# Attention, then experts, on one core: the values' product, three small transpositions and the output projection moved to other places in TensorE's order

## The reference

```python
def _stablemax3_s(x):
    pos = 1.0 + x * (1.0 + 0.5 * x * (1.0 + x / 3.0))
    neg = 1.0 / (1.0 - x * (1.0 - 0.5 * x * (1.0 - x / 3.0)))
    return jnp.where(x >= 0, pos, neg)
...
x = x + attention(layernorm(x))        # q, k, v, scores, stablemax3, values, output projection
h = silu(xn @ w1[e]) * (xn @ w3[e])    # xn = layernorm(x), four experts e, 512 wide
x = x + sum_e gates[:, e] * (h[e] @ w2[e])   # gates: softmax over the top 2 of 4
```

## Time and profile before

| | |
|---|---|
| time, median of 3 runs | 1129.02 us (1128.45 to 1129.56) |
| the profiled execution | 1130.74 us, of which 1129.0 us from the first instruction to the last |
| granted clock of TensorE, mean | 0.995 of full speed |
| instructions | 29283 |
| busy in the span | PE 98%, DVE 87%, ACT 89%, POOL 66% |
| DMA | 117.49 MB, mean 104 GB/s |

### The profile page before, as it was taken

The page is one execution under the profiler, slowest core; times in us unless marked ns, Lnnn a source line. Parts: engine busy times, 40 slices in busy tenths (PEclk is TensorE's granted clock), DMA queues, the critical chain, the costliest instruction groups (busy, mean ns, idle before and its releaser), DMA issues.

```text
span 1129.0 us, 29283 instructions
## 1 busy us (share of the span) xinstructions
PE 1104.0 (98%) x9968; PEld 936.7 (83%) x9968; DVE 980.8 (87%) x1789; ACT 1004.1 (89%) x1034; POOL 750.7 (66%) x999
## 2 busy tenths in 40 slices
PE   5889999999999999999999999999999999999998
PEld 4768888888888888888888888888888888888888
DVE  4878999999989999999899999999989899998844
ACT  0699999999999999999999999999999999999982
POOL 5346667776766777676687776677767668776530
PEclk8999999999999999999999999999999999999999
DMA  4534333333332233433323343223333322333100
GB/s 119 176 114 151 107 96 94 100 121 122 119 103 91 83 120 119 127 113 97 92 89 121 122 126 107 90 94 101 121 122 117 104 89 84 119 123 124 30 6 11
DMA packets 130127, 117.49 MB, mean 104 GB/s; under 512 B 15492, under 2 KB 124708, under 8 KB 130084
## 3 DMA queue, kind: packets, MB, share of 16 engines
q1 hardware_dynamic: 127876, 113.78, 32.3%
q10 hardware_dynamic: 2208, 3.15, 0.8%
HBM read 94.70 MB, written 21.09 MB: 103 GB/s over the span
## 4 chain that ended last, share of the span: by engine, by line
PE 90%; ACT 4%; DVE 3%; DMA 1%; issue 1%; ACTq 0%; SPq 0%; DVEq 0%
PE banks L1275 33%; PE banks L1548 20%; PE sc L1361 11%; PE banks L1293 10%; PE sc L1531 4%; PE misc L1275 2%; ACT poly L741 2%; PE banks L1582 2%; ACT poly L746 1%; PE misc L1408 1%; PE misc L1426 1%; PE misc L1386 1%; PE banks L1531 1%; PE sc L1275 1%; DVE mx L968 1%
## 5 line engine op out<-in xcount | busy, mean ns | idle before, releaser
L462 POOL TENSOR_TENSOR hid<-hid,gate_all 128x512 f32<-128x512 f32 x240 | 379.2, 1643 | 155.9 <-DMA gate_all<-gate_scratch 139.8
L883 DVE SCALAR_TENSOR_TENSOR poly<-w_sq,sc 128x1024 f32<-128x1024 f32 x252 | 303.7, 1216 | 37.6 <-ACT w_sq L637 37.5
L1275 PE MATMUL banks<-xn_hi,w_hi 128*128 128x256 f32 x976 | 289.3, 296 | 0.2
L1275 PE MATMUL banks<-xn_lo,w_hi 128*128 128x256 f32 x976 | 275.4, 282 | 0.0
L1275 PE MATMUL banks<-xn_hi,w_lo 128*128 128x256 f32 x976 | 274.2, 281 | 0.0
L637 ACT ACTIVATE w_sq<-sc 128x1024 f32<-128x1024 f32 x252 | 255.5, 1029 | 7.3 <-PE sc L1361 3.5
L741 ACT ACTIVATE poly<-poly,two 128x2048 f32<-128x2048 f32 x128 | 252.1, 1991 | 0.4
L1548 PE MATMUL banks<-w_sb,hid 128*128 128x128 f32 x1920 | 246.1, 281 | 0.2 <-POOL hid L462 0.2
L968 DVE TENSOR_REDUCE mx<-sc 128x4 f32<-128x1024 f32 x192 | 229.8, 1213 | 11.5 <-PE sc L1531 10.4
L1548 PEld LDWEIGHTS banks<-w_sb,hid 128*128 128x128 f32 x1920 | 223.3, 191 | 16.4 <-POOL hid L462 0.5
L746 ACT ACTIVATE poly<-poly 128x2048 f32<-128x2048 f32 x128 | 236.8, 1896 | 0.0
(11 more groups left out here) (186 smaller groups left out, 1372.5 us busy)
## 6 DMA issues: line engine op xcount, KB each, us to landing
qk_scratch<-qk_split SPq DMA_DIRECT2D x32, 512.0 KB, 3.1
k_tile<-qk_scratch SPq DMA_DIRECT2D x128, 128.0 KB, 2.5
q_pad<-qk_scratch SPq DMA_DIRECT2D x256, 64.0 KB
q_tile<-qk_scratch SPq DMA_DIRECT2D x124, 128.0 KB, 2.5
k_stack<-qk_scratch SPq DMA_DIRECT2D x124, 128.0 KB
gate_all<-gate_scratch SPq DMA_DIRECT2D x30, 512.0 KB, 4.4
x_in<-in_L_attn_x_dram SPq DMA_DIRECT2D x32, 128.0 KB, 2.1
x_res<-in_L_attn_x_dram SPq DMA_DIRECT2D x32, 128.0 KB, 2.2
```

The lines of the kernel that those rows point to most:

```text
L462: nc.gpsimd.tensor_tensor(h, h, by_token.unsqueeze(1).to_broadcast([128, 2, C, 128]), ALU.mult).then_inc(gated, 1)
L883: nc.vector.scalar_tensor_tensor(poly[:, u, :], w_sq[:, u % 2, :], 3.0, distance_buf(n, u), ALU.add, ALU.mult).then_inc(poly_ok, 1)
L1275: last = nc.tensor.matmul(dst, lhs[a], rhs[b], start=(k == 0), stop=(k == len(terms) - 1))
```

## The change

On TensorE, in the first half: `values` goes behind d0 and d1; `values_T` goes ahead of d4; b3 goes ahead of d5 (it stood behind it); `attention_T` leaves its place between d6 and a6 and goes to the end, ahead of `score(0)`. `output_projection` leaves the end of the first half and goes into the second, between `down(0, 0)` and `down(0, 1)`. On ACT the copy of attn_T leaves its place between square 6 and silu 6 and goes into the second half, behind the table load and ahead of the first logarithm. Instructions, sizes and buffers are the same; DVE's, POOL's and SP's orders are the same. It holds for the steps from 2 to 31.

```diff
@@ block.scalar
+            def attention_T_copied(i, off):
+                m = no(i, off) - 1
+                act.wait_ge(attnT_full, m + 1)
+                after(act, res_full, m)
+                nc.scalar.copy(attn_T[:], misc[:, 0:S]).then_inc(attnT_ok, 1)
...
                     square(6)
-                    attention_T_copied()
                     silu(6)
...
+                if settled(n):
+                    attention_T_copied(i, off)
                 if has(i, off):
                     log_of(0)
@@ block.tensor, first half
                 if settled(n):
-                    values()
                     distance(0)
                     distance(1)
+                    values()
                     weighted_values(i, off - 1, 3)
                     ups(1)
                     distance(2)
@@
                     distance(3)
                     up_b_unit(i, off - 2, 2)
                     up_a_unit(i, off - 2, 3)
+                    values_T()
                     distance(4)
-                    values_T()
                     up_a_unit(i, off - 2, 4)
+                    up_b_unit(i, off - 2, 3)
                     distance(5)
-                    up_b_unit(i, off - 2, 3)
                     up_b_unit(i, off - 2, 4)
                     up_a_unit(i, off - 2, 5)
                     distance(6)
-                    attention_T()
                     up_a_unit(i, off - 2, 6)
                     distance(7)
                     up_b_unit(i, off - 2, 5)
                     up_a_unit(i, off - 2, 7)
                     up_b_unit(i, off - 2, 6)
                     up_b_unit(i, off - 2, 7)
-                    output_projection()
+                    attention_T(i, off)
                     return
@@ block.tensor, second half
                 if settled(n):
                     score(0)
                     down(0, 0)
+                    output_projection(i, off)
                     down(0, 1)
                     score(1)
```

More of the change, by code:

```diff
@@ L669, in values_T_copied @@
                     nc.scalar.copy(o_T[:], pv).then_inc(o_ok, 1)
[L671 to L675, removed]
                 early = isinstance(i, int) and n == 1
@@ L1363, in distances, with attention_T, output_projection @@
                 last.then_inc(w_full, 1)
+            def attention_T(i, off):
+                n = no(i, off)
+                if not has(i, off - 1):
+                    return
+                m = n - 1
+                pe.wait_ge(attn_ok, m + 1)
+                for c in range(C):
+                    last = nc.tensor.transpose(misc[:, c * 128:(c + 1) * 128], attn[:, c, :], ident[:])
+                last.then_inc(attnT_full, 1)
+            def output_projection(i, off):
+                n = no(i, off)
+                if not has(i, off - 1):
+                    return
+                m = n - 1
+                pe.wait_ge(attnT_ok, m + 1)
+                for c in range(C):
+                    last = nc.tensor.matmul(misc[:, c * D:(c + 1) * D], attn_T[:, c * 128:(c + 1) * 128],
+                                            proj_T[:, 3, :], start=True, stop=True)
+                last.then_inc(res_full, 1)
             def first_half(i, off):
```

## The result

The changed kernel takes **1133.28 us** (median of 7 runs, 1132.55 to 1134.25) against 1128.81 us (median of 7 runs, 1128.44 to 1129.56) for the kernel before on the same chip: a ratio of 1.0038, 95% interval 1.0029 to 1.0048. That is 4.5 us slower and above the range given. The profiled execution's span is 1132.5 us (1129.0 before), at a granted clock of 0.997 (0.995 before), so the clock did not make it slower.

A forecast was written before the change was run, and what follows sets the result against it. The prediction took TensorE, 98% busy, to bound the kernel, losing time where loads wait. Its terms, 0.22 − 0.08 − 0.12 = +0.02 us a step, +0.6 us in 30 steps, gave 1129.6 us, range 1125.8 to 1132.8.

The forecast's parts named there:

- They keep step: DVE's adding of the result and later maxima some 0.2 us later, TensorE's later scores 0.22 us later: cost 0.
- the maxima's transfer: At d0, uncovered by moving the values' product: at most 0.03 us in every second step, 0 taken.
- The transpositions leave the gap: Between d6 and a6 their 0.22 us was free; ahead of the scores nothing covers them: +0.22 us a step.
- The projection: Moved between two blocks of D, it takes its 0.45 us there; the 0.09 us change to strips stays: sum 0.
- values_T −0.08 and b3 −0.12: Work ahead of d4 and d5 lets DVE's polynomials finish first: gains of 0.08 and 0.12 us a step.
- d4's sign: Profile sign if right: the next record behind d4 starts 0.46 us behind it.
- ACT's copy: Behind the table load, it lengthens ACT's stretch from silu 7 to square 2 by 0.27 us: cost 0, up to 0.05.
- ACT's stretch as the bound: Rival, chance 0.20: stretch 0.5 us longer, not 0.27, so b2 loses 0.13 us every step: +4.5 us, 1133.5 us.
- the margin that the forecast read for b2: At b2's load, waiting for a hidden: 0.15 us left beyond the semaphore's 0.04.
- The waits for the polynomials at d4 and d5: Rival, chance 0.06: these waits stay, DVE being as late as TensorE: +6.6 us, 1135.6 us.
- The faster rival: Chance 0.16: strip change runs under the transpositions at the end, a4 does not wait for silu 3: −3.6 us, 1125.4 us.
- No load hidden: Rival, chance 0.03: weight loads at d4 and d5 never overlap products, regaining some 0.04 us together: +5.4 us, 1134.4 us.

The follow-up runs named there:

- e5: Kernel before, with the two transpositions of attn done twice in the gap between d6 and a6: 1129.27 us against 1129.39, ratio 0.9999.
- e6: Kernel before, with a second pair of the transpositions at the end of the first half, ahead of the projection: 1135.64 us against 1129.39, ratio 1.0056.
- e7: Kernel before, with only the output projection moved behind the first block of D: 1130.17 us against 1129.39, ratio 1.0008.
- e2: Kernel before, with only values_T ahead of d4 and b3 ahead of d5: 1125.13 us against 1129.29, ratio 0.9966.
- e1: Kernel before, with only the values' product moved behind d0 and d1: 1130.04 us against 1129.29, ratio 1.0006.
- e4: Changed kernel with attention_T alone back between d6 and a6: 1129.83 us against 1129.29 for the kernel before, ratio 1.0006.
- e9: e4 with ACT's copy also back between square 6 and silu 6: 1126.38 us against 1129.06 for the kernel before, ratio 0.9974.

## Why the prediction was wrong

The forecast was +0.02 us a step, the measurement +0.137. The largest term was right. One step of the mechanism failed ("They keep step"), one price that had been seen was set to nothing (the maxima's transfer), and two gains were right in mechanism and too large. By the prediction's own terms:

- **The transpositions leave the gap: +0.22.** Right in mechanism and size: the gap kept its 1.19 us (1.20 in the changed kernel, 1.19 with the work doubled in e5), and the new place costs 0.22 us (P +0.223; e6 +0.216).
- **The projection: 0.** Right for TensorE: P does not change in e7 (5833 to 5834 ns).
- **values_T −0.08 and b3 −0.12: together −0.20.** Right in mechanism, over-sized: −0.152 (e2: −0.151 in the same piece). I had read one step. In the means of 27 steps, from a3's last product to a4's second it is 1.247 us before and 1.194 after, so values_T gave 0.053 and not 0.08; d5 takes 0.565 before and 0.463 after, so b3 gave 0.102 and not 0.12. The work of values_T was also counted as 0.44 us, where the rows have 0.36 (531.88 to 532.24) and 0.35 (532.34 to 532.69). That changed nothing, since the chain through silu 3 is longer than the work either way. The same chain is why d4's sign, 0.46 us to the next record, did not come (0.552 in the mean).
- **DVE's adding: "They keep step: 0."** This step of the argument failed. Its own figures have the projection end at 543.1, 0.1 us behind the 543.00 at which the adding started, and say "some 0.2 us later" without a source for the other 0.1. The adding stood directly behind the first maximum, with no wait, 2.34 us behind b7's last product (540.66 to 543.00). In the changed kernel it is 2.61 (541.51 to 544.12): the projection ends about where the forecast had it (543.38 + 0.61 = 543.99), and DVE, which now waits for it, starts 0.13 us after that. In the means, against b7's last product, the adding is 0.265 us later, the maximum behind it 0.274, and TensorE's second scores 0.227. DVE falls 0.047 us behind TensorE, in e7 0.048. TensorE waits for the last maximum: M +0.032 (e7: +0.036). It does so in every second step above all, where M was 0.07 us longer already before; in the others there is slack, and M grows by 0.009.
- **The values' product: 0, "0.03 us at most, in every second step".** The price was seen and then dropped, and it was too small: in every second step, as said, but 0.05 us, which is 0.023 in the mean (e1: 0.024). Nothing stands against it: no later piece became shorter.
- **ACT's copy: 0.** Right. The stretch grew by 0.27 us, and b2 is not late (1442 before, 1436 after).
- The last 0.014 us is spread over the other pieces and P.

The miss is 0.137 − 0.02 = 0.117 us a step, 3.5 us in 30 steps: 0.048 of gains that were too large, 0.032 of DVE's adding, 0.023 of the maxima's transfer and 0.014 of the rest. None is larger than 0.05 us, and all lay on the slow side. Each had been rounded to a gain or to nothing; whether more than chance put them all on one side, the runs can't say.

**The rivals.** ACT's stretch as the bound would have given 1133.5 us, almost the measured time, and it is not the cause: in the changed kernel d2 takes 462 ns and b2 with a3 1436, as before. A time that fits proves no mechanism. The mechanism exists, though. e4 and e9 show it at 0.09 us a step, near the 0.13 that the rival had worked out, once TensorE is not later itself. It comes as 0.17 us in every second step, though, and not as 0.13 in each: the margin that the forecast read for b2 holds in one step of two. The waits for the polynomials at d4 and d5 did not stay (T). The faster rival needed the change to strips under the transpositions; it stayed outside, at 0.09 us. No load hidden: e2 rules it out. For M, DVE's falling behind by 0.05 us is shown with and without the rest of the change; an order in which DVE adds later, behind another maximum, was not tried.

## What to carry to other kernels

Ask what a wait's length is tied to before moving work out of it. When the chain behind it starts at an instruction ahead of the gap, work inside is free as long as it is shorter than the wait, and taking it out gains nothing and pays in full where nothing covers it (e5 against e6: the same 0.22 us, 0 or 6.3 us). What shortens such a wait is to begin its chain earlier: a5 ahead of b4 is worth another 0.17 us a step, some 5 us, on top of e2 (33,059 to 32,885 ns). And in a loop of 30 steps on a full engine, terms of 0.02 to 0.05 us decide: average each over many steps instead of reading one, look whether the steps alternate, and put a margin, not a zero, on what "keeps step".

## What the runs showed of the hardware that I had not expected

- From the end of a product's record (an end that is modelled) to the start of the DVE instruction that waits for it: 0.13 us (543.99 to 544.12, and in the mean of 25 steps). From DVE's end to a waiting weight load it is 0.06 us (561.14 to 561.20, e4).
- A weight load can be late by more than it costs: in e4 b2's load was held for 0.24 us, and from d3 to the second product of b2 it took 0.66 us (560.76 to 561.42) instead of 0.58 undisturbed (0.46 and 0.12): 0.08 us.
- Going from the whole array to strips of 32 rows costs 0.09 us in both places measured: 0.54 against 0.45 us for the projection (0.537 and 0.447 in the means), 0.31 against 0.22 for the transpositions.
